# One graph-attention layer on one core: a ring of three weight halves, products by halves, ten row buffers

## The reference

```python
feat = concat([xn[src], xn[dst]], axis=1)                 # 8192 x 2048
e_f  = concat([relu(feat[:256] @ W_hh + b_hh), relu(feat[256:1536] @ W_oo + b_oo), relu(feat[1536:] @ W_ho + b_ho)])
logit = e_f @ W_a + b_a                                   # one number for each edge
alpha = softmax of logit over the edges with the same dst
z = segment_sum(alpha * xn[src], dst)
gnn = relu(concat([xn, z], 1) @ (W_hn for rows 0-127, W_on for the others) + b)
mix = linear attention of xn (16 heads; q, k by elu + 1; v), then @ w_proj + b_proj
x = x + gnn + mix
out = x + bitlinear(gelu(bitlinear(layernorm(x))))        # 1024 -> 128 -> 1024, 8-bit activations, ternary weights
```

## Time and profile before

| what | us |
|---|---|
| median of 3 runs (786.36 to 787.28) | 787.23 |
| the profiled execution | 785.15 |
| its span, first to last instruction | 783.4 |
| PE busy | 660.7 |
| DVE busy | 505.2 |
| ACT busy | 209.5 |
| POOL busy | 259.7 |
| mean granted clock of TensorE | 0.923 of full speed |

### The profile page before, as it was taken

One profiled execution on the slowest core, in us unless ns is written; L12 is line 12 of the kernel. 1 busy time (PEld: TensorE's weight loads), 2 busy tenths in 40 slices (PEclk: granted clock), 3 DMA queues, 4 the chain that ended last, 5 costly groups with the idle time before them and its releaser, 6 DMA issues. The chain is left out here.

```text
span 783.4 us, 8227 instructions
## 1 busy us (share of the span) xinstructions
PE 660.7 (84%) x2739; PEld 467.8 (60%) x2741; DVE 505.2 (64%) x1084; ACT 209.5 (27%) x266; POOL 259.7 (33%) x191
## 2 busy tenths in 40 slices
PE   4999999999847997798999699999955676798952
PEld 3778887788735775575778456677710011586621
DVE  8968813635645556365764597865568896327996
ACT  4333322220332354041614425152220100311001
POOL 3000306655654206247475555401223000002340
PEclk9999999999988999798999999999995779899985
DMA  9753449999999768969999999945360023140201
GB/s 347 257 203 135 141 184 298 296 323 320 323 303 317 269 200 226 306 200 312 306 287 296 317 318 236 303 151 189 108 242 0 0 80 135 54 140 5 108 27 80
DMA packets 41721, 163.40 MB, mean 209 GB/s; under 512 B 5168, under 2 KB 5552, under 8 KB 34512
## 3 DMA queue, kind: packets, MB, share of 16 engines
q0 software_dynamic: 20160, 73.41, 36.1%
q1 hardware_dynamic: 20800, 88.88, 30.1%
q10 hardware_dynamic: 720, 0.59, 0.2%
HBM read 146.08 MB, written 16.78 MB: 208 GB/s over the span
## 5 line engine op out<-in xcount | busy, mean ns | idle before, releaser
L1384 PE MATMUL bank_low<-w_hi,xT_hi 128*128 128x512 f32 x496 | 201.7, 407 | 8.2 <-DVE w_lo L861 3.2
L1385 PE MATMUL bank_low<-w_lo,xT_hi 128*128 128x512 f32 x496 | 196.4, 396 | 0.0
L1386 PE MATMUL bank_low<-w_hi,xT_lo 128*128 128x512 f32 x496 | 196.2, 396 | 0.0
L560 POOL DMA_INDIRECT gathered_rows<-edge_tables,dst_row x68 | 115.8, 1703 | 76.8 <-DMA gathered_rows<-edge_tables,src_row 65.5
L1029 DVE SCALAR_TENSOR_TENSOR gathered_rows<-gathered_rows,wa_bc 128x1024 f32<-128x1024 f32 x68 | 83.0, 1221 | 83.1 <-DMA gathered_rows<-edge_tables,dst_row 83.1
L560 POOL DMA_INDIRECT gathered_rows<-edge_tables,src_row x68 | 87.0, 1279 | 127.2 <-DVE gathered_rows L1029 91.8
L861 DVE TENSOR_TENSOR w_lo<-w_raw,w_hi 128x2048 fp32r<-128x2048 f32 x48 | 107.9, 2288 | 31.2 <-ACT w_hi L633 30.9
L1384 PEld LDWEIGHTS bank_low<-w_hi,xT_hi 128*128 128x128 f32 x496 | 95.3, 192 | 38.0 <-issue 12.3
L1386 PEld LDWEIGHTS bank_low<-w_hi,xT_lo 128*128 128x128 f32 x496 | 95.0, 191 | 20.6
L1385 PEld LDWEIGHTS bank_low<-w_lo,xT_hi 128*128 128x128 f32 x496 | 95.2, 192 | 18.7
L633 ACT ACTIVATE w_hi<-w_raw 128x2048 fp32r<-128x2048 f32 x50 | 92.8, 1902 | 8.3 <-DMA w_raw<-in_wt 8.3
(11 more groups left out here) (269 smaller groups left out, 951.7 us busy)
## 6 DMA issues: line engine op xcount, KB each, us to landing
w_raw<-in_wt SPq DMA_DIRECT2D x54, 1024.0 KB, 8.2
edge_tables<-stage SPq DMA_DIRECT2D x32, 256.0 KB, 7.1
x_in<-in_x SPq DMA_DIRECT2D x4, 512.0 KB, 9.1
xn_scratch<-xn SPq DMA_DIRECT2D x4, 512.0 KB, 4.6
node_top<-stage SPq DMA_DIRECT2D x8, 256.0 KB, 7.7
x_part<-in_x SPq DMA_DIRECT2D x8, 256.0 KB, 5.5
mix_out<-stage SPq DMA_DIRECT2D x8, 256.0 KB, 2.0
xn_raw<-xn_scratch SPq DMA_DIRECT2D x4, 512.0 KB, 5.8
```

The costliest lines, as they stand in the source:

```text
L560: pool.indirect_dma_start(rows_sum[:, s, :], None, table_d[0:rows, :], bass.IndirectOffsetOnAxis(ap=index[:, t:t + 1].bitcast(U32), axis=0 ...
L1384: pe.matmul(dest, lh, rh, start=start and i == 0, stop=False)
L1385: pe.matmul(dest, lh, rl, start=False, stop=False)
L1386: last = pe.matmul(dest, ll, rh, start=False, stop=last_one)
```

## The change

The diff names the target rows "added by the DMA"; in the kernel before they are added by the DMA as well, and the gather code is the same but for names. What differs:

- `w_hi` and `w_lo` are rings of three halves in place of four. Half h of chunk c lies in slot (2c+h) mod 3. Only the last half, (BON1, 1), lies elsewhere.
- PE goes over all row tiles of a chunk with the first half of it, then over all with the second (`chunk_product`). The four banks are thus filled side by side, and the results of a chunk come out in its second half. Chunk 0 keeps the old order.
- ACT splits half (c+1, 0) when chunk c-1 is finished and half (c+1, 1) when the first half of chunk c is (`first_halves`), then makes the copies of chunk c. SP loads (c+2, 0) before the stores of chunk c and (c+2, 1) after them.
- The freed 16 KB of each partition are four more row buffers: `SLOTS` is 10.
- DVE works single tiles (`edge_tile`), the maximum of a tile behind the mask of the next (`catch_up`), and `TILES` gives the number of tiles behind `w_lo` of (c, 1) and of (c+1, 0): 13 in the table chunks, 8 in the HH chunks (before: 4), 34 from K0 to ON1, 13 in PR0. All 36 early maxima are read in PR1.
- `kv_product`, `den8` and `attend` move to other places between the halves, and with them their parts on ACT and DVE. DVE's kq sums stand at the end of a chunk.

```diff
 
-PAIRS = {4: 2, 5: 3, 6: 2, 7: 3, HHT0: 1, HHT1: 1, K0: 3, V0: 3, HN1: 1, K1: 3, V1: 3, Q0: 2, Q1: 3, ON0: 3, ON1: 1}
-assert sum(PAIRS.values()) * 2 == T_GATHERED
-MAXIMA = {PR0: (0, 18), PR1: (18, 36)}
+RING = 3
+TILES = {5: (2, 2), 6: (2, 3), 7: (2, 2), HHT0: (1, 1), HHB0: (1, 1), HHT1: (1, 1), HHB1: (1, 1),
+         K0: (2, 2), HN0: (1, 0), V0: (2, 2), HN1: (1, 1), K1: (2, 2), V1: (2, 2), Q0: (2, 2), Q1: (2, 2),
+         ON0: (2, 1), ON1: (2, 2), PR0: (2, 11)}
+assert sum(map(sum, TILES.values())) == T_GATHERED
+MAXIMA = {PR1: (0, 36)}
 T_EARLY = 36
-SLOTS = 6
+SLOTS = 10
+LAG = 2
 LOADED = 4
+
...
+       [("q", 1, j) for j in range(4)] + [("z", 1, j) for j in range(4)]
+
+ATTEND = {(Q1, 1, 0): [(0, 0), (0, 1)], (Q1, 1, 1): [(0, 2), (0, 3)], (ON0, 1, 0): [(1, 0), (1, 1)], (ON0, 1, 2): [(1, 2), (1, 3)]}
+DEN8 = {(Q1, 0, 2): 0, (ON0, 0, 1): 1}
+KV_AT = {(HN1, 0, 0): 0, (Q0, 0, 0): 1}
 
 
...
-    w_hi = sb("w_hi", [P, 2, KT * CW], F32R, at_w_hi)
+    at_w_hi = region(RING * HALF * 4)
+    w_hi = sb("w_hi", [P, RING, HALF], F32R, at_w_hi)
     bhn1 = sb("bhn1", [P, 2, HALF], F32, at_w_hi)
-    w_lo = sb("w_lo", [P, 2, KT * CW], F32R)
+    w_lo = sb("w_lo", [P, RING, HALF], F32R)
...
-    at_big = region(32768)
+    at_big = region(32768 + 16384)
     x_in = sb("x_in", [P, MT, D], F32, at_big)
     xn = sb("xn", [P, MT, D], F32, at_big + 16384)
-    rows_sum = sb("gathered_rows", [P, SLOTS, D], F32, at_big)
+    rows = sb("gathered_rows", [P, SLOTS, D], F32, at_big)
...
+    def w_half(c, h):
+
+        if (c, h) == (BON1, 1):
+            return last_hi[:, :], last_lo[:, :]
+        slot = (2 * c + h) % RING
+        return w_hi[:, slot, :], w_lo[:, slot, :]
...
+        def load_next(c, h):
+            sp.wait_ge(w_lo_done, 2 * (c - 1) + h + 1)
+            load_half(c, h)
+            if h == 0 and c in BIASED:
+                sp.wait_ge(bias_lo_done, bias_no(c))
+                load_bias(bias_no(c))
+
         for c in range(TABLES):
-            for h in range(2):
-                sp.wait_ge(w_lo_done, 2 * (c + 1) + h + 1)
-                load_half(c + 2, h)
-            if c + 2 in BIASED:
-                sp.wait_ge(bias_lo_done, bias_no(c + 2))
-                load_bias(bias_no(c + 2))
+            load_next(c + 2, 0)
             for m in range(MT):
                 store(4 * c + m + 1, m % 2, table_tiles[c // 2, m, :, (c % 2) * CW:(c % 2 + 1) * CW])
+            load_next(c + 2, 1)
...
+        def hi_half(c, h):
+
+            if h == 0:
+                act.wait_ge(prod_ready, FIRST[c - 1] + HEAD)
+                if c in BIASED:
+                    n = bias_no(c)
+                    act.wait_ge(bias_loaded, n * 32 + 32)
+                    act.activation(b_hl[0:64, n % 2, :], b_raw[0:64, :], ACT.Copy).then_inc(bias_hi_done, 1)
+            elif c == BON1:
+                act.wait_ge(prod_ready, FIRST[BON0] + HEAD)
+            else:
+                act.wait_ge(first_halves, c)
+            act.wait_ge(raw_loaded[h], 16 * (c + 1))
+            act.activation(w_half(c, h)[0], raw[:, h, :], ACT.Copy).then_inc(w_hi_done, 1)
...
+            for c in range(4 * i, 4 * i + 4):
+                hi_half(c + 1, 0)
+                if c == 0:
                     transposed_hi(3)
+                hi_half(c + 1, 1)
                 for m in range(MT):
-                    evac_stage(i * 16 + (4 * cc + m), m % 2, i * 128 + 16 * ((4 * cc + m) // 2), m)
+                    evac_stage(4 * c + m, m % 2, 16 * ((4 * c + m) // 2), m)
...
         for c in range(TABLES, BON0):
-            split_chunk(c + 1)
             if c == HHT0:
                 split_feat(1)
+            hi_half(c + 1, 0)
+            if c == K0:
+                copy_mlp_weights()
+            if c == K1:
+                copy_kv(0)
+            if c == Q0:
+                copy_kv(1)
+            if c != PR1:
+                hi_half(c + 1, 1)
+            if c == Q1:
+                for j in range(4):
+                    attend(0, j)
+            if c == ON0:
+                for j in range(4):
+                    attend(1, j)
...
+            if c == PR1:
+                hi_half(BON0, 1)
...
 
-        def edge_pair(t):
+        def edge_tile(t):
 
             if t % LOADED == 0:
+                catch_up()
                 load_blocks(t)
-            for u in range(2):
-                s = (t + u) % SLOTS
-                mask_others(t + u)
-                dve.wait_ge(dst_added[s], 16 * ((t + u) // SLOTS + 1))
-                dve.scalar_tensor_tensor(out=rows_sum[:, s, :], in0=rows_sum[:, s, :], scalar=0.0, in1=wa_bc[:, :], op0=ALU.max, op1=ALU.mult,
-                                         accum_out=logit[:, t + u:t + u + 1]).then_inc(edge_dot, 1)
-            for u in range(2):
-                dve.wait_ge(edge_dot, t + u + 1)
-                take_max(t + u)
+            s, landed = t % SLOTS, 16 * (t // SLOTS + 1)
+            mask_others(t)
+            row = rows[:, s, :]
+            catch_up()
+            dve.wait_ge(dst_landed[s], landed)
+            dve.scalar_tensor_tensor(out=row, in0=row, scalar=0.0, in1=wa_bc[:, :], op0=ALU.max, op1=ALU.mult,
+                                     accum_out=logit[:, t:t + 1]).then_inc(edge_dot, 1)
+            behind.append(t)
+
+        behind = []
+
+        def catch_up():
+            if behind:
+                take_max(behind.pop())
 
...
 
         for c in range(TABLES, PR1 + 1):
-            split_chunk(c + 1)
-            work = []
             if c == HHT0:
                 split_feat(1)
-            if c in (HHB0, HHB1):
-                work = [lambda i=i, half=int(c == HHB1): hh_logits(half, i) for i in range(2)]
+            lo_half(c, 1)
             if c == K0:
                 finish_hh()
 
                 dve.memset(kvb[:, :, :], 0.0).then_inc(kv_cleared, 1)
                 dve.memset(vbuf[:, :, :, P:P + 1], 1.0).then_inc(kv_cleared, 1)
-            if c in (K0, K1):
-                work = [lambda j=j, a=int(c == K1): add_kq("k", a, j) for j in range(4)]
             if c == K1:
                 spread_ks(0)
+            edge_work(c, 0)
             if c == Q0:
                 spread_ks(1)
-                work = [lambda j=j: add_kq("q", 0, j) for j in range(4)]
-            if c == Q1:
-                work = [lambda: add_kq("q", 1, 0), lambda: invert_den(0), lambda: add_kq("q", 1, 1), lambda: add_kq("q", 1, 2),
-                        lambda: attend(0, 0), lambda: attend(0, 1), lambda: add_kq("q", 1, 3), lambda: attend(0, 2), lambda: attend(0, 3)]
-            if c == ON0:
-                work = [lambda: invert_den(1), lambda: attend(1, 0), lambda: attend(1, 1)]
-            if c == ON1:
-                work = [lambda: attend(1, 2), lambda: attend(1, 3)]
-            edge_work(c, work)
+            if c in (Q1, ON0):
+                a = int(c == ON0)
+                invert_den(a)
+            lo_half(c + 1, 0)
+            if c in (Q1, ON0):
+                for j in range(4):
+                    attend(int(c == ON0), j)
+            edge_work(c, 1)
+            if c in (HHB0, HHB1):
+                for i in range(2):
+                    hh_logits(int(c == HHB1), i)
+            if c in (K0, K1):
+                for j in range(4):
+                    add_kq("k", int(c == K1), j)
+            if c in (Q0, Q1):
+                for j in range(4):
+                    add_kq("q", int(c == Q1), j)
+            if c == PR0:
+                catch_up()
             if c in MAXIMA:
                 take_maxima(*MAXIMA[c])
+        lo_half(BON0, 1)
 
...
+        def first_chunk():
+
+            for m in range(MT):
+                pe.wait_ge(evac_done, m + 1)
+                for h in range(2):
+                    last = half_product(m, 0, h, m, xT, h == 0, False, lambda k: wait_first(m, k))
+                    if m == MT - 1 and h == 0:
+                        last.then_inc(first_halves, 1)
                 pe.wait_ge(bias_lo_done, 1)
-                last = pe.matmul(bank[b][:, :], ones_b[:, :], b_hl[0:64, bias_slot, :], start=False, stop=True)
-            return last
+                add_bias(m, 0, False, True).then_inc(prod_ready, 1)
+
+        def chunk_product(c, lhs, before=None):
+
+            for h in range(2):
+                pe.wait_ge(w_lo_done, 2 * c + h + 1)
+                for i, m in enumerate(ROWS[c]):
+                    b = bank_of[c, i]
+                    if h == 0:
+                        free(c, i)
+                        if c in BIASED:
+                            pe.wait_ge(bias_lo_done, bias_no(c) + 1)
+                            add_bias(b, c, True, False)
+                    if c in (Q0, Q1):
+                        last = half_product_q(b, c, h, i)
+                    else:
+                        last = half_product(b, c, h, m, lhs, h == 0 and c not in BIASED and c not in (HHB0, HHB1),
+                                            h == 1 and c not in (HHT0, HHT1), before if i == 0 else None)
```

(13 more changed lines are left out.)

229 lines of the change are left out of this document (85 added, 144 removed).

## The result

The kernel after takes 794.3 us (median of 4 runs, 792.4 to 798.0) against 786.8 for the kernel before beside it (786.2 to 787.3): ratio 1.0106, 95% interval 1.0082 to 1.0130. It is slower by 7.5 us (the two profiled executions differ by 10.2: 795.4 and 785.15). The forecast was 777, faster; the direction was wrong, and 794.3 lies inside the range of 760 to 798. The profiled execution has a span of 793.6.

The account below looks back on a forecast made before the run. TensorE was taken to bound the main stage, DVE the part from 573.9 us. PR0 would start at 485 for 522, the hot stage at 564 for 573.9, 10 us less: 777, own range 767 to 786, over all 760 to 798.

Parts of the forecast that it names:

- What bounds the kernel: Main stage bound by TensorE, with 40.4 us of waits and 9 from half clock, about 49; from 573.9 DVE bounds.
- (a): Main stage: 13 tiles for 20 in table chunks, 8 for 4 in HH, with ten buffers; part of removing 49 us.
- (b): Main stage: each half's split asked for half a chunk early, single tiles between; feat_dst_lo, den8, `stage`, most b_hl and w_lo go.
- The waits left in the main stage: PE still waits 4 us over the four HH chunks, 4 around HN0, 4 in ON0: together 12.
- The clock: Main stage: lower clock after the remaining waits costs 2 us.
- moved attends: Main stage: the moved attends shed about 2 us of small waits, so PR0 starts at 485 in place of 487.
- The supply sum: From 116 us to V1's end: 40 tiles and about 17 chunks need 168 + 95 = 263 us of DMA in 254.
- Rival B: Table chunks: copies out through `stage` become the bound, deciding from stores of 12 us; 796 with stores of 13; chance 0.22.
- The tail: From PR0's start s: late tiles, reduction, adds, copy at s+43, PE stands 12 us, maxima; hot stage at s+79 = 564.
- `edge_max` is full at s+37: PR0, s being its start: lo (PR1,0) by s+12.6, then 11 tiles in 24 us, last tile's maximum at s+37.
- rival C: PR0's 11 tiles wait for rows, 5.1 us each for 2.2, 32 us more: 807 or so; chance 0.08.
- The 4 us of contention: PR1's four POOL adds fall into DVE's 36 maxima, 4 x 1.05 = 4 us on top of 22.

Follow-up runs that it names:

- the best kernel found with ring, halves and ten buffers: The kernel after with 8 of PR0's 13 tiles moved earlier and DVE's split of (BON0,0) put behind the 36 maxima: 766.1 us, ratio 0.9741.

## Why the prediction was wrong, point by point

- *What bounds the kernel: right.* "About 49 us of the main stage are no work": whole-chunk splits with moved tiles start PR0 49.4 us earlier, 40.6 of it fewer idle us of PE and 8.8 shorter busy time, for the 40.4 and 9 of the prediction.
- *Which part removes it: half wrong.* I gave it to (a) fewer tiles ahead of the splits and (b) the halves. (a) is all of it; the rest of the change, with (b) in it, gives 3 us alone and takes 20 back on top of (a).
- *The waits left in the main stage: right in sum, by luck.* 12 predicted, 12.2 measured, but HH 6.5 for 4, HN0 and V0 3.1 for 4, ON0 2.6 for 4; and 4.8 of the 6.5 came from feat_dst_lo ahead of a split, which the prediction had let go whole. *The clock: mis-sized,* 2 for some 6. The 2 us that I took off for moved attends did not show. Together PR0 at 492 for 485. That matmul work is unchanged was nearly right: PR0 takes 24.7 us in both kernels, and up to PR0 the 2 us left over above are all that could belong to it.
- *DMA: right.* Its share stays full through 280 to 340 us; the first gather is issued at 116.6, as supposed (116). The supply sum came to 263 us in 254, 9 short, and was called just enough.
- *Rival B did not occur.* The 16 table stores in the window of the earlier trace rows now land in 6.6, 7.2 and 7.4 us at the least, median and most, and ACT's longest wait for one is 6.8. What I drew from the Trainium skill (DMA: Bandwidth & Descriptors, "Queues, rings and completion order"), that gathers would hold the stores at 9.8 or more wherever they are issued, gave the wrong figure: apart from the loads they landed faster with the DMA as full. B's mechanism, a held `stage`, is nonetheless what lost the time, only in the tail and in the 4.8 us of HHT0.
- *The tail: the failed step.* "POOL reduces in 1.8, and only then adds": the add came 7.1 us after the reduction, the change of POOL's work, a term that I had at nothing. The trace of before could not show it, as POOL there waited 20.5 us for x_part and had its change under that wait; I priced it from a row that hid it, and set no bound. The reduction itself took 3.9 for 1.8, beside DVE's split. And "`edge_max` is full at s+37" was s+45: (PR1,0) was split at s+14.6 for s+12.6, since ACT's copy ahead of it stood 11.45 us for a store of ON's results, and the 11 tiles waited some 6.5 us for rows between 520 and 536. I had excluded that, since ten buffers would be full; it is rival C's mechanism at a fifth of its price. So ACT's copy came at s+59.5 for s+43, PE stood 28.1 for 12, and DVE had its split at s+63 for s+48.5.
- *The 4 us of contention:* PR1's four adds met the maxima only in part; these took 22.9 us, not 26. Where POOL's adds did meet them, in the run with the maxima ahead of the split, it was 26.2.
- *The sum.* First one-hot 564 predicted, 584 measured: 7 from PR0's start, 8 from late rows and the late split of (PR1,0), 9 from the reduction and POOL's change, less some 4 on what follows. None of the three turned the direction by itself: with the largest, the 9, taken off, it would be some 785, an estimate, and so within 0.2% of before.

## What to carry to other kernels

Change the places of the work before its grain: here one line that moves tiles gave 22 to 24 us, and the best kernel found with ring, halves and ten buffers was no faster. A deferred piece of work costs what hangs on its end, so follow the chain behind the last deferred item engine by engine, and count every queue in which something unrelated stands behind it. On POOL, price a change between gathers, adds and a reduction at 7 to 8 us unless a long wait covers it, and look at what DVE runs beside it. A row that shows a wait bounds nothing that may lie under the wait.

## What the hardware showed that was not expected

- POOL stands 6.6 to 8.5 us at each exposed change between indirect DMAs, tensor_tensor and partition_all_reduce, with "issue" as the releaser, and nothing between two operations of one kind. Waits of 7.6 us or more on DVE or a load left nothing of it to see. Shorter ones cover less: in the run with the tiles of before the row says 9.84, ACT's copy was ready 7.4 us behind the reduction, and the add came 2.4 later still. The change from gathers to the reduction was never seen uncovered.
- A reduction of 1.80 us takes 3.88 when DVE's `w_lo` split of 2.29 us starts 0.08 us ahead of it, in all eight runs where they meet, and adds of 1.25 took 2.6 to 2.8 in three runs; the maxima beside POOL's adds show the same from DVE's side, 1.3 for 0.35.
